# Counting edges of a graph network: edge units moved towards the first blocks, and twenty of twenty-five blocks put into a hardware loop on two engines

## The reference

```python
row, col = (edge_index[0], edge_index[1])
def spmm(feat):
    msg = feat[col] * w[:, None]
    return jax.ops.segment_sum(msg, row, num_segments=n)
for _ in range(K):                       # K = 10
    out = spmm(out) * BETA + h * ALPHA
...
h = x @ W                                # two GCN layers sum over the same edges
out = jax.ops.segment_sum(h[src] * norm[:, None], dst, num_segments=n)
```

```python
h = jax.nn.relu(edge_attr @ W_edge + b_edge)          # (100000, 96)
mu = jnp.mean(h, axis=0)
var = jnp.mean(jnp.square(h - mu), axis=0)
```

## Time and the profile before

| what | value |
|---|---|
| median of 3 runs | 2522.56 us (2520.0 to 2524.38) |
| the profiled execution | 2522.56 us, of which its span is 2520.8 us |
| `count_edges` in the span | 50 to 574 us |
| all copies of the windows, L691 | 200, from 86.1 to 568.9 us |
| mean granted clock of TensorE | 0.763 of full speed |

### The profile page before, as it was taken

How to read it: one execution, slowest core, us unless ns; L and a number is a source line. 1 busy time by engine, 2 the same in 40 slices (tenths; PEclk the granted TensorE clock), 3 DMA queues, 4 the chain that set the end, 5 groups by cost and what they waited for, 6 DMA issues and landing times. The chain is left out here.

```text
span 2520.8 us, 47900 instructions
## 1 busy us (share of the span) xinstructions
PE 1816.2 (72%) x13986; PEld 1424.6 (57%) x13986; DVE 1553.1 (62%) x4128; ACT 876.7 (35%) x1637; POOL 915.8 (36%) x1183
## 2 busy tenths in 40 slices
PE   1777777778999999959852766666566666655488
PEld 0334444448999999955542644444444444444477
DVE  7888876665544444455544866666666666666743
ACT  4478876654111111112121433333333333332420
POOL 3321211220200000000016777777777777777100
PEclk9999998789999999979965555555555555555799
DMA  4312111110000000260012222222222222222200
GB/s 135 122 60 69 59 66 62 62 56 20 2 2 2 1 2 2 91 256 1 2 43 42 67 58 59 59 58 58 60 59 58 60 59 58 59 60 50 71 2 20
DMA packets 87663, 134.28 MB, mean 53 GB/s; under 512 B 48866, under 2 KB 56674, under 8 KB 87480
## 3 DMA queue, kind: packets, MB, share of 16 engines
q1 hardware_dynamic: 41416, 84.79, 9.9%
q0 software_dynamic: 25344, 38.98, 7.7%
q10 hardware_dynamic: 20720, 8.06, 1.5%
HBM read 97.15 MB, written 34.58 MB: 52 GB/s over the span
## 5 line engine op out<-in xcount | busy, mean ns | idle before, releaser
L1496 POOL DMA_INDIRECT counts<-p_rows,rows x784 | 745.6, 951 | 302.9 <-issue 238.7
L1725 PE MATMUL ps_e_z<-e_w_q,counts 128*128 128x96 f32 x1568 | 362.2, 426 | 89.3 <-issue 85.2
L1725 PEld LDWEIGHTS ps_e_z<-e_w_q,counts 128*128 128x128 f32 x1568 | 341.3, 330 | 123.6 <-issue 115.9
L593 DVE TENSOR_TENSOR hot_w<-iota_w,places_now 128x1600 f16<-128x1600 f16 x300 | 297.0, 990 | 127.8 <-PE ps_counts L619 97.9
L619 PE MATMUL ps_counts<-hot_w,hot_p 128*128 x1196 | 274.5, 359 | 125.0 <-DVE hot_p L593 94.1
L1736 PE MATMUL ps_e_seg<-counts 128*128 128x192 f16 x784 | 140.4, 359 | 277.9 <-DVE counts L1553 277.8
L1736 PEld LDWEIGHTS ps_e_seg<-counts 128*128 128x128 f16 x784 | 100.8, 138 | 362.6 <-DVE counts L1536 342.4
L1673 ACT ACTIVATE counts<-ps_e_z 128x768 f16<-128x768 f32 x98 | 79.5, 811 | 627.0 <-DVE ps_e_z L1542 624.8
L1542 DVE TENSOR_TENSOR ps_e_z<-ps_e_z,counts 128x768 f32<-128x768 f32 x98 | 94.7, 967 | 310.2 <-DMA counts<-p_rows,rows 298.5
L979 PE MATMUL ps_hop<-y_even,counts 128*128 128x192 f16 (+1 forms) x3125 | 264.7, 246 | 7.7 <-DVE y_even L833 6.9
L979 PEld LDWEIGHTS ps_hop<-y_even,counts 128*128 128x128 f16 x3125 | 263.1, 98 | 8.6 <-DVE y_even L833 7.0
(11 more groups left out here) (407 smaller groups left out, 2490.0 us busy)
## 6 DMA issues: line engine op xcount, KB each, us to landing
counts<-count_rows SPq DMA_DIRECT2D x30, 800.0 KB, 6.6
count_rows<-staged SPq DMA_DIRECT2D x25, 800.0 KB, 3.3
counts<-p_rows,rows POOLq DMA_INDIRECT x784, 2.5
e_attr<-attr_parts SPq DMA_DIRECT2D x99, 72.0 KB
attr<-attr_parts SPq DMA_DIRECT2D x50, 140.6 KB
e_dst_rows<-dst_row SPq DMA_DIRECT2D x99, 64.0 KB
e_w_q<-q_rows ACTq DMA_DIRECT2D x392, 12.0 KB
attr_parts<-staged SPq DMA_DIRECT2D x6, 784.0 KB, 14.9
```

The lines of the kernel that those rows point to most:

```text
L593: made = nc.vector.tensor_tensor(hot[:, s, :, :].rearrange("p j (e t) -> p j e t", t=2), iota_w[:, 0:n].rearrange("p (e t) -> p e t", t=2) ...
L1496: nc.gpsimd.indirect_dma_start(z[:, slot, j, :], None, k.p_rows, bass.IndirectOffsetOnAxis(rows, 0)) \
L1725: mm = pe.matmul(ps_z[:, two, j // (STEP_TILES // 2), at:at + D], u_hot[:, two, j * P:(j + 1) * P], w_q[:, fed, j // Q_TILES, :], start=Tr ...
```

## The change

The change does four things.

1. The units are spread anew: 7, 7, 6, 5, 5 in the first five blocks and one in each of the other twenty.
2. The order within a block is simpler. In the first five blocks each window (the second to the last window of block 0, the first windows of the others) has one unit, and it is multiplied, rectified and squared there, all after one window. In the other blocks the unit is multiplied in window 2, rectified in window 3 and squared in window 5, as the single unit was before.
3. Blocks 5 to 24 run in a hardware loop of 10 turns with two blocks each on SyncE and ScalarE, so there the block number is a register, and so are semaphore values and addresses worked out from it. TensorE stays written out for all 25 blocks, with constants.
4. SyncE loads a unit in the block that uses it, behind the store of the block before, and no longer one unit ahead. The load of `x` moves from block 4 to the front of the stage, ahead of the first unit's load.

```diff
-    UNITS = [7, 4, 4, 4, 4, 4, 3, 3, 2, 2] + [1] * 13 + [0] * 2
-    PLACES = {0: (), 1: ((2, 3, 5),), 2: ((0, 1, 3), (4, 5, 7)), 3: ((0, 1, 2), (2, 3, 5), (5, 6, 7)),
-              4: ((0, 1, 2), (2, 3, 4), (4, 5, 6), (6, 7, 7)),
-              7: tuple((j, j, j) for j in range(1, 8))}
+    EARLY = [7, 7, 6, 5, 5]
...
         def units_of(d):
-            first = sum(UNITS[0:d])
-            return [(first + n,) + at for n, at in enumerate(PLACES[UNITS[d]])]
+            early = len(EARLY)
+            if isinstance(d, int) and d < early:
+                first = sum(EARLY[0:d])
+                return [(first + n, n + (d == 0)) for n in range(EARLY[d])]
+            return [(d + (sum(EARLY) - early), 2)]
+
+        def for_blocks(eng, one_block):
+            early = len(EARLY)
+            for d in range(early):
+                one_block(d, d % 2)
+            with eng.Fori(0, (NB - early) // 2) as two:
+                for odd in (1, 0):
+                    one_block(two * 2 + (early + 1 - odd), odd)
...
             def one_block(d, odd):
-                for n, _, _, _ in units_of(d):
-                    if n + 1 < U_UNITS:
-                        sp.wait_ge(u_done, n + 1)
-                        load(n + 1)
-                if isinstance(d, int) and d == 4:
-                    load_x(sp, k, k.x, x_in)
-                    sp.dma_start(k.x[LAST:P, NB - 1, :], k.named["x"][0:P - LAST, :]).then_inc(x_in, 16)
+                for n, _ in units_of(d):
+                    if not isinstance(n, int) or n:
+                        sp.wait_ge(u_done, n)
+                    load(n)
                 sp.wait_ge(window_out, d * WINDOWS + (WINDOWS + 2))
-                sp.dma_start(k.count_rows[d, :, :],
+                sp.dma_start(k.count_rows[bass.ds(d, 1), :, :].rearrange("a p e -> (a p) e"),
...
             sp.wait_ge(k.parts_stored, 16 * 9)
+            load_x(sp, k, k.x, x_in)
+            sp.dma_start(k.x[LAST:P, NB - 1, :], k.named["x"][0:P - LAST, :]).then_inc(x_in, 16)
             sp.wait_ge(ones_set, 1)
-            load(0)
-            for d in range(NB):
-                one_block(d, d % 2)
+            for_blocks(sp, one_block)
...
-                out = nc.scalar.copy(k.counts[:, lo:hi, d, :],
+                out = nc.scalar.copy(k.counts[:, lo:hi, bass.ds(d, 1), :].rearrange("p b a s -> p b (a s)"),
                                      turned_in(n % 2, hi - lo))
...
-                    for n, _, taken, squared in units:
-                        if taken == j:
+                    for n, at in units:
+                        if len(units) > 1 and j == at:
                             rectified(n)
-                        if squared == j:
                             squares(n)
-
-            for d in range(NB):
-                one_block(d, d % 2)
+                        elif len(units) == 1 and j == at + 1:
+                            rectified(n)
+                        elif len(units) == 1 and j == at + 3:
+                            squares(n)
+
+            for_blocks(act, one_block)
```

More of the change, by code:

```diff
@@ L454, in count_edges @@
     PARTS = [(0, 7), (7, 13), (13, 19), (19, NB)]
-    UNITS = [7, 4, 4, 4, 4, 4, 3, 3, 2, 2] + [1] * 13 + [0] * 2
-    PLACES = {0: (), 1: ((2, 3, 5),), 2: ((0, 1, 3), (4, 5, 7)), 3: ((0, 1, 2), (2, 3, 5), (5, 6, 7)),
-              4: ((0, 1, 2), (2, 3, 4), (4, 5, 6), (6, 7, 7)),
-              7: tuple((j, j, j) for j in range(1, 8))}
-    assert sum(UNITS) == U_UNITS and len(UNITS) == NB
+    EARLY = [7, 7, 6, 5, 5]
+    assert sum(EARLY) + NB - len(EARLY) == U_UNITS and len(EARLY) % 2 == 1
     DEGREE = BANK - 64
@@ L642, in edges @@
                 pe.wait_ge(attr_in, n * 16 + 16)
-                if n:
+                if not isinstance(n, int) or n:
                     pe.wait_ge(u_taken, n)
@@ L661, in one_block @@
                         turn(d - 1, 1 - odd, j // 2)
-                    for n, multiplied, _, _ in units:
-                        if multiplied == j:
+                    for n, at in units:
+                        if at == j:
                             edges(n)
@@ L697, in turn @@
                 act.wait_ge(turned, d * len(PARTS) + (n + 1))
-                out = nc.scalar.copy(k.counts[:, lo:hi, d, :],
+                out = nc.scalar.copy(k.counts[:, lo:hi, bass.ds(d, 1), :].rearrange("p b a s -> p b (a s)"),
                                      turned_in(n % 2, hi - lo))
                 if n == len(PARTS) - 1:
-                    out = nc.scalar.activation(k.deg_in[:, d:d + 1], ps_t[:, n % 2, DEGREE:DEGREE + 1], ACT.Copy,
+                    out = nc.scalar.activation(k.deg_in[:, bass.ds(d, 1)], ps_t[:, n % 2, DEGREE:DEGREE + 1], ACT.Copy,
                                                scale=2.0)
@@ L706, in rectified @@
                 act.wait_ge(u_done, n + 1)
-                if n:
+                if not isinstance(n, int) or n:
                     act.wait_ge(u_summed, n)
                 nc.scalar.activation(u[:, :, :], ps_u[:, :, 0:U_EDGES], ACT.Relu,
-                                     accum_out=u_sums[:, 0, n:n + 1]).then_inc(u_taken, 1)
+                                     accum_out=u_sums[:, 0, bass.ds(n, 1)]).then_inc(u_taken, 1)
             def squares(n):
@@ L714, in squares @@
                 nc.scalar.activation(u[:, :, :], u[:, :, :], ACT.Square,
-                                     accum_out=u_sums[:, 1, n:n + 1]).then_inc(u_summed, 1)
+                                     accum_out=u_sums[:, 1, bass.ds(n, 1)]).then_inc(u_summed, 1)
             def one_block(d, odd):
@@ L720, in one_block @@
                     window(d, odd, j)
-                    if j % 2 == 0 and d:
+                    if j % 2 == 0 and not (isinstance(d, int) and d == 0):
                         turn(d - 1, j // 2)
-                    for n, _, taken, squared in units:
-                        if taken == j:
+                    for n, at in units:
+                        if len(units) > 1 and j == at:
                             rectified(n)
-                        if squared == j:
                             squares(n)
-            for d in range(NB):
-                one_block(d, d % 2)
+                        elif len(units) == 1 and j == at + 1:
[3 more added lines that the diff above has]
+            for_blocks(act, one_block)
             for n in range(len(PARTS)):
```

2 lines of the change are left out of this document (1 added, 1 removed).

## The result

The changed kernel takes 2564.47 us (median of 4 runs, 2559.85 to 2571.14), beside 2523.47 us (4 runs, 2520.0 to 2526.61) for the kernel before on the same chip. The ratio is 1.0166, with a 95% interval of 1.0143 to 1.0187: 41.0 us slower by the medians, where 39.4 were forecast. The profiled execution took 2558.31 us, 35.8 us more than that of before, and its blocks account for 35.0 of those 35.8.

What follows compares the result with a forecast made beforehand. VectorE was taken to bound block 0, VectorE and ScalarE to be nearly full in blocks 2 to 4, GpSimd's windows to floor late blocks. 2522.6 + 30 + 6.5 - 4 + 2.5 + 4 gave 2562 us, range 2537 to 2588.

Steps and rivals of the forecast that it cites:

- The units in blocks 1 to 4: Blocks 1 to 4: ScalarE's own work for 23 units instead of 16 sums to 123.9 against 106.3 us, 17.6 more.
- The whole term of 30: Blocks 1 to 4 together: 17.6 us for units, 11 for load stalls, 1 for last windows, 30 us more.
- The 1 us for the last windows: Blocks 3 and 4: last windows have no unit and follow each other at TensorE's pace, 1 us more in all.
- The loads, 11 us: Starts of blocks 2, 3 and 4: the unit's load lands late behind the store, ScalarE stands 3.7 us each time.
- The load of `x`: Block 0: the load of x ahead of the first unit's load delays that unit, 6.5 us more (5.4 to 8).
- Blocks 5 to 9: With 8 units fewer, these blocks fall to GpSimd's floor, 100.5 against 105.0 us: 4 us less (0 to 4.5).
- Registers: Blocks 5 to 24, ScalarE and SyncE: worked-out waits and addresses delay late hand-overs, 0.2 us a block, 4 us more.
- The last two blocks: Blocks 23 and 24 get a unit each, from 28.2 us for both: 2.5 us more (1 to 6).
- Loads in time: Rival: TensorE finds its unit data in time, so without 11 us of stalls 2551 us; chance 0.15.
- Code loading: Rival: each of 10 loop jumps back costs a code fetch of 2.6 us, 26 more, 2588 us; chance 0.06.
- The slow cadence: Rival: all 15 last blocks run 17.1 us long at TensorE's lower clock, 23 us more, 2578 us; chance 0.13.
- Idle time filled: Rival: added units only fill ScalarE's idle time and late blocks run at 14.64 us: 2518 us; chance 0.06.

Runs made afterwards that it cites:

- units_spread: Changed kernel with value ranges, loads one unit ahead, x back in block 4, early units spread over the windows and squared one window after the ReLU: 2578.55 us.
- before_bounded: The kernel before with a stated range on each value read from window_tabs on TensorE and GpSimd: 2571.04 us, ratio 1.0213.
- loads_ahead_2: The changed kernel with the same value ranges as before_bounded and unit loads one unit ahead again, x staying in front: 2594.60 us.
- late_written_out: Changed kernel with value ranges, loads ahead and x in block 4 (2587.91 us), with blocks 5 to 24 written out on SyncE and ScalarE: 2589.58 us.
- units_packed: before_bounded with its own unit numbers, but units in each block's first windows, rectified after the matmul's window and squared at once: 2598.59 us.

## Why the prediction was right, point by point

**The total.** 2562 us was forecast and 2564.5 measured, slower at 0.93. The signs and the causes named for the early blocks and for `x` were right: units, late loads and `x` each cost time there, and the steps back show it. That the total came out within 2 us is in part luck. In the profile the early blocks cost 2.4 us more than forecast and blocks 5 to 9 gave 3.1 less, while blocks 10 to 22 came out 4.4 us shorter for no cause that is shown, where 4 more were forecast for registers.

**The units in blocks 1 to 4, 17.6 us.** With the other parts undone, what is left costs 15.4 us there (units_spread to before_bounded, one profile each); it is mostly the numbers, with what still differs in the order. The whole term of 30 measured 32.4. The sum behind the 17.6 was too large, though: it had 123.9 us of ScalarE's own work in these blocks, and ScalarE was busy 36.82 + 80.64 = 117.5. The block lengths were forecast as 39, 35, 31 and 31 us and came out as 37.75, 34.64, 33.36 and 32.92: less in block 1, more in the tail.

**The 1 us for the last windows** is the term that was mis-sized most. I had put "no idle time of ScalarE at all" under the sum, and on top of it 11 us for the stalls and 1 us for the tails. ScalarE was busy 117.5 of 138.7 us, so it idled 21.2 us, not 12. The error in its work and the one in its idle time offset each other. By the test written down, it should show no idle time in block 2 beyond the first 6 us; there it was busy 27.63 of 28.64 us, which is 1 us short of the letter of the test. It idles more in blocks 3 and 4. The order costs 4.6 us in blocks 1 to 4 and another 4.9 in 5 to 9, by one profile of each kernel on the bounded base.

**The loads, 11 us.** 3.7 us for each of three stalls. The load came at T + 4.85, where T + 4.4 was forecast and the bounds were 3.0 and 5.9. The store itself lands 3.8 us after its issue with a load behind it, for 3.3 without, so the two transfers overlap in part, and the load's data can be used 1 us after the store's landing. The Trainium skill (DMA: Bandwidth & Descriptors, section Queues, rings and completion order) has the signal of a transfer land only after every earlier write of that transfer engine, while the data themselves may finish out of order. The trace agrees with the first, 4.85 us for the load behind 3.8 for the store; no run here shows the second. The step that failed was TensorE being "a window ahead" at each turn, at T + 1: it reached the unit's matmuls early at block 2 (169.3, T + 0.7), and not at blocks 3 and 4 (T + 3.0 and T + 3.6), ahead of which two and three windows had no unit. So 7.4 us of waits, not 10.5, and with the loads ahead again blocks 1 to 4 gave back 4.3. The waits inside the blocks, 6.8 us, were not in the sum, and loading ahead does not end them: in loads_ahead_2 the unit matmuls of blocks 1 to 4 still stand 3.5 us for data and 4.8 us for ScalarE, since there is one buffer and a unit in every window. All late loads together are 8.6 us on the bounded base.

**The load of `x`, 6.5 us.** Block 0 by the last copy went from 74.3 to 80.8 us, and undoing it gave 6.7 us. The first unit's wait, forecast at "about 6" us, was 6.88. This was the best worked term.

**Blocks 5 to 9, 4 us less.** They gave 0.9. They lost nine units and not eight, 14 less 5 (the matmuls went from 606 to 570, 36 fewer), and a unit frees 1.13 us of TensorE and not 4 x 0.406, as the matmuls overlap: 10 us in all. The floor was a shade high, as blocks 10 and 11 of the kernel before took 14.5 us for the 14.64 worked out, and even so its 100.5 us were not reached: TensorE's clock fell from 0.98 to 0.93, and it was busy 76.64 us where 81.00 less 10 would be 71. On the bounded base units_spread had these blocks 8.1 us under before_bounded.

**Registers, 4 us more, and the late blocks.** At a late turn of the changed kernel, open bank and copy:

```profile
435.27 0.21 PE L618 MATMUL ps_counts<-zeros_h,ident_h 128*128 128x2 f16 x1
...
435.63 0.50 ACT L697 ACTIVATE staged<-ps_counts 128x400 f16<-128x400 f32 x1 [1.80 <-PE ps_counts L618]
```

The copy starts 0.15 us after the matmul's end. Of some 95 copies in blocks 5 to 24 before which ScalarE stood, only 20 have a gap over 0.1 us (0.12 to 0.17), the first copy of each block; the others have 0.04 to 0.07 us, as with constants, so it seems that most waits are worked out ahead. With the loop written out these gaps were gone and nothing that can be told was won. SyncE issues its load 0.62 to 0.92 us after the store in the loop and 0.42 before it, and no unit waits for that. The term was nil within what the runs can tell. Blocks 10 to 22 were even 4.4 us shorter: the earlier trace rows had a clock of 0.84 and 157.08 us of TensorE there, and now it is 0.87 and 151.57 for the same 1222 instructions. There are two fewer blocks of 17 us or more, three for five. Nothing in the change is shown to cause it.

**The last two blocks, 2.5 us more:** 1.7.

**The rivals.** Loads in time: out, they were waited for 21.0 us. Code loading: out, as neither instruction queue moved more packets and late_written_out won nothing. The slow cadence: not in the late blocks for which it was written, but the clock did fall in the early ones, from 1.00 to 0.81, and no rival had that. The Trainium skill (TensorE: Matmul & The Clock Gate, section HAM oscillation) tells of waits for data that send TensorE back to its lower clock; this trace agrees, with 1.90 us for four unit matmuls after the wait of 4.18. I had not weighed that rule. Idle time filled: its mechanism may be half true. With the order nearly kept, moving units towards the front cost 15.4 us and gave 8.1 back in the two profiles; the net is near what one can tell from nothing.

## What to carry to other kernels

A sum of one engine's own work says what a block can't go under, not what it takes: ask for each gap of the neighbour what this engine has queued in that moment. In units_packed the same work in the same blocks cost 24 to 28 us more only because it was packed into the first windows. ScalarE then stood for TensorE in the windows without a unit, up to 4.98 us, and TensorE's clock was lower, 0.78 for 0.90 in blocks 5 to 9. And a load that is issued one use ahead has its slack for nothing as long as the uses lie apart: behind an 800 KB store on the same queue it comes 4.85 us after the store is issued.

## What the runs showed of the hardware that was not expected

- Instructions of an engine's sequencer are not free in a short loop. Thirteen more on TensorE in a loop over batches of four matmuls (with 999 in all on GpSimd, which was hardly waited for) took the kernel from 2517 to 2839 us. Two more for each table value, on TensorE and GpSimd, took it to 2571; which of the two engines made that was not tried. The profile shows such time as "issue", and in the first case the granted clock stood at 0.50 in late blocks, so the batches themselves took 1.67 us for 0.85.
- TensorE's clock was at the lower level after single waits of 4.18 and 6.88 us (four unit matmuls at 1.90 us for 1.04), in blocks where the kernel before had it at 1.00 throughout. After the waits of 1.82 and 1.36 us the four matmuls still took 1.04 us, and the clock fell within the two batches behind them (2.70 us for some 1.6 in block 3).
- A hardware loop of ten turns with two blocks each on SyncE and ScalarE cost nothing that could be measured. The instruction queue q8 moved the same 116 packets, and q14 64 for 67.
- With a 141 KB load 0.4 us behind it on the same queue, an 800 KB store landed 3.8 us after its issue for 3.3 alone, and the load's data were used 4.83 to 5.0 us after the store's issue, once 5.79.
